# Two attention-and-MoE streams on one core: batch 1 projected while slot 0 loads, maxima of group 0 between the last expert blocks, results sent from two queues

## The reference

```python
x = x + 0.5 * ffn(layernorm(x))
x = x + attn(layernorm(x))        # 16 heads of 8, 4 kv heads, rotary
x = x + 0.5 * ffn(layernorm(x))

def ffn(x):
    x = x + softmax(q @ k.T / sqrt(8)) @ v @ w_proj     # q, k, v from layernorm(x) * w + b
    onehot = one_hot(argmax(layernorm(x) @ gate_w + gate_b), 8)
    return x + onehot-chosen expert: gelu(x @ w1[e]) @ w2[e]
```

## Time and profile before

| | |
|---|---|
| median of 3 runs | 1563.21 us (1561.63 to 1566.58) |
| the profiled execution | 1566.45 us |
| its span, first to last instruction | 1564.7 us |
| mean granted TensorE clock | 0.962 |
| busy: TensorE, VectorE, ACT, GpSimd | 1406.8, 1185.5, 1124.5, 639.8 us |

### The profile page before, as it was taken

One profiled execution on the slowest core, in us unless ns is written; L12 is line 12 of the kernel. 1 busy time (PEld: TensorE's weight loads), 2 busy tenths in 40 slices (PEclk: granted clock), 3 DMA queues, 4 the chain that ended last, 5 costly groups with the idle time before them and its releaser, 6 DMA issues.

```text
span 1564.7 us, 35538 instructions
## 1 busy us (share of the span) xinstructions
PE 1406.8 (90%) x12228; PEld 687.4 (44%) x12228; DVE 1185.5 (76%) x1945; ACT 1124.5 (72%) x2148; POOL 639.8 (41%) x972
## 2 busy tenths in 40 slices
PE   2899999999999886999999999999999999999895
PEld 1333334333339773333333333333334343334885
DVE  5788888888855254888888888888888888894532
ACT  1478887788785452778888887888887878787553
POOL 2422344542226555333544453233324543213753
PEclk8699999999999986999999999999999999999998
DMA  4344333533102315323322333332333233211243
GB/s 119 95 111 114 103 100 108 132 94 95 47 26 60 105 49 154 96 77 93 94 80 68 98 95 101 93 82 67 93 94 82 73 99 99 60 38 37 72 113 104
DMA packets 101423, 137.60 MB, mean 88 GB/s; under 512 B 29664, under 2 KB 72032, under 8 KB 101248
## 3 DMA queue, kind: packets, MB, share of 16 engines
q1 hardware_dynamic: 70864, 85.82, 19.1%
q0 software_dynamic: 24000, 45.04, 12.0%
q10 hardware_dynamic: 6384, 4.47, 1.0%
HBM read 79.05 MB, written 53.51 MB: 85 GB/s over the span
## 4 chain that ended last, share of the span: by engine, by line
PE 55%; DVE 31%; issue 6%; POOL 2%; DMA 2%; SPq 2%; ACT 1%; DVEq 0%; ACTq 0%; POOLq 0%
DVE maxima L1210 26%; PE banks L851 14%; PE banks L839 11%; PE banks L823 11%; PE banks L878 3%; PE banks L1554 3%; PE banks L860 3%; PE banks L1563 3%; PE banks L904 1%; PE banks L885 1%; SPq L463 1%; POOL by_token L1537 1%; DVE stats L1287 1%; DVE split L1218 1%; POOL sorted_x L691 1%
## 5 line engine op out<-in xcount | busy, mean ns | idle before, releaser
L1210 DVE TENSOR_REDUCE maxima<-banks 128x2 f32<-128x1024 f32 x768 | 924.2, 1222 | 171.9 <-PE banks L823 166.8
L1181 ACT ACTIVATE work<-banks 128x512 f32<-128x512 f32 x1536 | 829.3, 597 | 149.2 <-PE banks L839 135.2
L823 PE MATMUL banks<-K,Q 64*128 64x512 f32 x1536 | 572.7, 463 | 56.3 <-DVE maxima L1210 36.4
L839 PE MATMUL banks<-Q,K 64*128 64x512 f32 x1536 | 567.7, 451 | 0.6
L851 PE MATMUL banks<-work,V 128*9 128x256 f32 x6144 | 476.8, 382 | 1.6 <-ACT work L1181 0.8
L823 PEld LDWEIGHTS banks<-K,Q 64*128 64x128 f32 x1536 | 229.9, 190 | 214.6 <-DVE maxima L1210 126.4
L839 PEld LDWEIGHTS banks<-Q,K 64*128 64x128 f32 x1536 | 229.3, 186 | 181.7 <-issue 137.4
L851 PEld LDWEIGHTS banks<-work,V 128*9 128x9 f32 x6144 | 91.5, 88 | 276.1 <-issue 204.5
L710 POOL TENSOR_TENSOR lo<-full,hi 128x512 fp32r<-128x512 f32 x42 | 53.7, 1278 | 251.7 <-ACT hi L1059 144.4
L1617 DVE COPY work<-w 128x512 f32 x88 | 43.7, 497 | 87.2 <-PE banks L1554 75.5
L1563 PE MATMUL banks<-w,work 128*128 x736 | 102.3, 284 | 2.5 <-issue 1.3
(11 more groups left out here) (187 smaller groups left out, 1331.8 us busy)
## 6 DMA issues: line engine op xcount, KB each, us to landing
Q<-q_scratch SPq DMA_DIRECT2D x188, 128.0 KB, 2.6
K<-k_scratch SPq DMA_DIRECT2D x376, 64.0 KB, 2.4
Q<-zero_rows SPq DMA_DIRECT2D x182, 64.0 KB, 2.2
q_scratch<-hi POOLq DMA_DIRECT2D x42, 256.0 KB, 4.7
q_scratch<-lo POOLq DMA_DIRECT2D x42, 256.0 KB, 6.8
k_scratch<-hi POOLq DMA_DIRECT2D x21, 256.0 KB, 4.6
k_scratch<-lo POOLq DMA_DIRECT2D x21, 256.0 KB, 6.8
work<-sorted_x SPq DMA_DIRECT2D x76, 66.0 KB, 1.9
```

The costliest lines, as they stand in the source:

```text
L823: fill(nc.tensor.matmul(bank, q4[parts(j), n % SLOTS, j // 2, qt * P:(qt + 1) * P], k4[parts(j), n % SLOTS, j // 2, :], start=True, stop=T ...
L839: nc.tensor.matmul(scp[x % EXPS][:, :], k4[parts(j), n % SLOTS, j // 2, kt * P:(kt + 1) * P], q4[parts(j), n % SLOTS, j // 2, :], start=Tr ...
L1181: nc.scalar.activation(prob[:, kt, j ^ 1, :], scp[x % EXPS][:, :], ACT.Exp, scale=SCALE).then_inc(s.probs, 1)
L1210: nc.vector.tensor_reduce(c.maxima[:, at:at + 9:8], c.banks[:, k * S:(k + 2) * S].rearrange("p (m n) -> p m n", m=2), AX.X, ALU.max).then_ ...
```

## The change

**Opening of stream 0.** `BETWEEN` is gone: batch 1 is projected right behind batch 0 (`SECOND` in both streams), in tiles of its own (`apart(1)` now holds in both), and the maxima of group 0 close the opening. VectorE norms batch 1 ahead of the low parts of batch 0. Only slot 0 of `K`, `Q` and all of `V` are set in `setup`; the rest of `Q` and `K` and `empty` follow later. GpSimd, not ACT and SP, issues the straight loads of `K`. ACT issues its stores between its copies for batch 1. The statistics of batch 2 (`norms(-2, kt)`, first in VectorE's `main`) come behind the maxima of group 0, in both streams.

**Change of streams.** The maxima of group 0 of stream 1 move from behind the expert blocks into the opening's generator: one quarter ahead of each of the last three blocks, the fourth behind. SP clears and loads slot 0 from block 20 on.

**Finish.** VectorE adds half of Y to X during the last blocks; one pass for each batch is left. Loads and stores of the last four batches alternate between SP and ACT.

```diff
@@ setup, gpsimd
-            nc.gpsimd.memset(c.empty[:, :, :], 0.0)
-            nc.gpsimd.iota(c.empty[:, :, D].bitcast(U32), pattern=[[P, 2 * E]], base=NT * P, channel_multiplier=1)
+            nc.gpsimd.memset(c.V[:, :], 1.0)
+            nc.gpsimd.memset(cols(c.K, 0, KSLOT).bitcast(F32), -1.0)
@@ setup, vector
+            nc.vector.memset(cols(c.Q, 0, KSLOT).bitcast(F32), 0.0)
@@ Plan
-        for n, kt in SECOND if ahead else ():
+        for n, kt in SECOND:
             self.group(n, kt)
         self.maxima(0)
         for qt in range(QT):
             self.put([("max", 1, qt, j) for j in range(J)])
-            for n, kt in () if ahead else BETWEEN[qt]:
-                self.group(n, kt)
@@ sync, opening
-                    sp.wait_ge(c.q_clear, 1)
-                    sp.wait_ge(c.k_clear, 1)
...
-                    yield from pause(NBLK - RINGX)
+                    yield from pause(EARLY_AT + 16 - RINGX)
                     clear_rows(0)
                 whole_ready(sp, 0, 0)
                 yield from straight(sp, 0, 0)
-                for i in range(2):
+                for i in range(1 + label):
                     sp.wait_ge(s.lo[i], 1)
                     yield from straight(sp, i, 1)
@@ gpsimd, opening
-                    nc.gpsimd.memset(c.K[:, :].bitcast(F32), -1.0).then_inc(c.k_clear, 1)
-                    nc.gpsimd.memset(c.V[:, :], 1.0).then_inc(c.v_clear, 1)
+                    whole_ready(pool, 1, 0)
+                    yield from straight(pool, 1, 0)
+                    pool.wait_ge(s.lo[1], 1)
+                    yield from straight(pool, 1, 1)
+                    nc.gpsimd.memset(cols(c.K, KSLOT, (SLOTS - 1) * KSLOT).bitcast(F32), -1.0).then_inc(c.k_clear, 1)
+                    for i in range(2):
+                        low_part(i, 1)
+                    link(nc.gpsimd.memset(c.empty[:, :, :], 0.0))
+                    nc.gpsimd.iota(c.empty[:, :, D].bitcast(U32), ...).then_inc(c.empty_ready, 1)
@@ tensor, opening
-                for n, kt in FIRST + (SECOND if label else ()):
+                for n, kt in FIRST + SECOND:
                     group(n, kt)
                     if label:
                         yield
+                loaded(0)
+                for qt in range(QT):
+                    maxima(0, qt)
+                    if label:
+                        yield
@@ scalar, opening
+                if label == 0:
+                    group(-8, 0)
+                    roots(1)
+                    group(-8, 2)
+                    group(-6, 0)
+                    group(-6, 2)
+                    group(-4, 0)
+                    for i in range(2):
+                        yield from store(act, i, 0, s.first_stored[i], (0,))
+                    group(-4, 2)
+                    group(-2, 0)
+                    group(-2, 2)
@@ scalar, main
+                for i in range(2):
+                    stored(act, i, 2)
@@ vector, opening
-                    nc.vector.memset(c.Q[:, :].bitcast(F32), 0.0).then_inc(c.q_clear, 1)
+                    yield from early(1)
                     for i in range(2):
                         low_first(i)
-                    yield from early(1)
+                    nc.vector.memset(cols(c.Q, KSLOT, (SLOTS - 1) * KSLOT).bitcast(F32), 0.0).then_inc(c.q_clear, 1)
...
+                    yield from pause(4)
+                for qt in range(QT):
+                    for half in range(2):
+                        take_max(0, qt, half)
+                    if label:
+                        yield
@@ finish, vector
+        for b in range(B):
+            x, y = cols(c.X, b * S, S), cols(c.Y, b * S, S)
+            nc.vector.scalar_tensor_tensor(out=x, in0=y, scalar=0.5, in1=x, op0=ALU.mult, op1=ALU.add).then_inc(s.halved, 1)
+            yield
-            nc.vector.tensor_tensor(n, n, y, ALU.add).then_inc(s.summed, 1)
-            dve.wait_ge(s.summed, b + 1)
             nc.vector.scalar_tensor_tensor(out=x, in0=n, scalar=0.5, in1=x, op0=ALU.mult, op1=ALU.add)\
                 .then_inc(s.combined, 1)
```

More of the change, by code:

```diff
@@ L405, in apart @@
         def apart(b):
-            return label > 0 and b == 1
+            return b == 1
         def full(b):
@@ L638, in main @@
                             load_outputs(sp, c, b)
+                    if n == 1 and later:
+                        sp.wait_ge(c.empty_ready, 1)
                     if n >= 1 and later:
@@ L752, in main @@
                         norm(EARLY)
-                    if label and n < 0:
+                    if n < 0:
                         continue
@@ L1005, in main @@
                     pe.wait_ge(blocks.s.out_copied, HALVES * NBLK)
-                loaded(0)
-                for qt in range(QT):
-                    maxima(0, qt)
                 turn_max(0)
@@ L1012, in main @@
                     maxima(1, qt)
-                    for n, kt in () if label else BETWEEN[qt]:
-                        group(n, kt)
                 for n in range(last):
@@ L1145, in opening @@
                     yield from pause(EARLY_AT + 4)
-                for n, kt in FIRST:
-                    group(n, kt)
-                    if label:
-                        yield
-                group(-5, 0)
-                whole_ready(act, 1, 0)
-                if label == 0:
-                    act.wait_ge(c.k_clear, 1)
-                    yield from send_first()
-                else:
+                if label == 0:
+                    group(-8, 0)
[9 more added lines that the diff above has]
+                    group(-2, 2)
+                else:
+                    for n, kt in FIRST:
+                        group(n, kt)
+                        yield
+                    group(-5, 0)
+                    whole_ready(act, 1, 0)
                     sending = send_first()
@@ L1632, in finish, with send @@
 def finish(nc, c, ctx, out, blocks):
-    s = sems(ctx, nc, "fin", "summed combined stored")
+    s = sems(ctx, nc, "fin", "halved combined stored")
     ahead = B // HALVES
+    def send(eng, b):
+        eng.wait_ge(s.combined, b + 1)
+        eng.dma_start(out[b].rearrange("(t p) d -> p t d", p=P), by_token(cols(c.X, b * S, S))).then_inc(s.stored, 16)
     def sync(sp):
@@ L1643, in sync @@
         blocks.all_stored(sp, 4 * NBLK)
-        for b in range(ahead, B):
+        for b in range(ahead, B, 2):
             load_outputs(sp, c, b)
+        for b in range(ahead, B, 2):
+            send(sp, b)
     def vector(dve):
-        yield from pause(EARLY_AT)
+        for b in range(B):
+            x, y = cols(c.X, b * S, S), cols(c.Y, b * S, S)
+            nc.vector.scalar_tensor_tensor(out=x, in0=y, scalar=0.5, in1=x, op0=ALU.mult, op1=ALU.add).then_inc(s.halved, 1)
+            yield
         for b in range(B):
@@ L1661, in scalar @@
     def scalar(act):
-        yield from pause(EARLY_AT + 1)
-        for b in range(B):
-            if b == ahead:
-                yield from pause(NBLK)
-            elif b < ahead:
-                yield from pause(2)
-            act.wait_ge(s.combined, b + 1)
-            act.dma_start(out[b].rearrange("(t p) d -> p t d", p=P), by_token(cols(c.X, b * S, S))).then_inc(s.stored, 16)
+        yield from pause(RINGX + 1)
+        for b in range(ahead):
+            yield from pause(2)
+            send(act, b)
+        yield from pause(NBLK)
+        blocks.all_stored(act, 4 * NBLK)
+        for b in range(ahead + 1, B, 2):
+            load_outputs(act, c, b)
+        for b in range(ahead + 1, B, 2):
+            send(act, b)
         act.wait_ge(s.stored, 16 * B)
```

39 lines of the change are left out of this document (19 added, 20 removed).

## The result

The changed kernel takes 1556.16 us (median of 10 runs, 1553.59 to 1561.75), the kernel before beside it 1563.65 us (10 runs). The ratio is 0.9954, 95% interval 0.9939 to 0.9969: **faster, by 7.2 us**, where 20.5 were forecast.

A forecast was written before the change was run, and what follows sets the result against it. The chain was 55% TensorE, 31% VectorE; with steady steps unchanged, gains lay in waits at three places. 10.6 + 8.3 + 1.6 = 20.5 us off 1566.45 gave 1545.95, less 3.2 for the median: 1543, range 1538 to 1551.

The forecast's parts named there:

- Opening, up to the first max matmul: Start of stream 0: first max matmul at 29.8 in place of 34.45, 4.6 us earlier.
- The stall (2.8 us): Opening: batch 0's first tensor_scalar, 2.95 us long until GpSimd's memset of K ends, would lose 2.8 us.
- I keep the 5.5 us: Opening: from the last slot 0 load issue to the first max matmul, 5.5 us would pass as before.
- The check on TensorE: Opening: first max matmul can't precede the end of batch 1's matmuls, at 26.2 or up to 3 us later.
- Opening, from there to the first scores: First max matmul to the first exponential's scores: 21.2 us in place of 27.2, 6.0 us earlier.
- What could be late next: Opening: slot 1's stores go out earlier and have ten us of first maxima, so no wait was counted.
- ACT's wait: Opening: ACT waits for batch 1's stores before its first exponential; landed by 45, scores come at 51.
- Slot 1 sets it instead: Change of streams: slot 1's load sets group 1's start, 608.8 in place of 617.13, 8.3 us earlier.
- land 6.9 us later as before, plus 0.8: Change of streams: slot 1's scratch stores, out at 595.5, land at 603.2; 0.8 allows for 768 KB more beside GpSimd's.
- the stores still catch slot 0 or slot 1 at the change of streams: Rival: group 1 starts 3 us earlier, not 8; 15.2 us saved, 1548; chance 0.13.
- the one for the opening: Rival: slot 0 lands no earlier in the opening; 15.9 us saved, 1547; chance 0.14.
- both together: Slot 0 no earlier in the opening and stores catching a slot at the change of streams: 1553, chance 0.04.

The follow-up runs named there:

- after: The changed kernel itself, all three parts of the change, against the kernel before: 1556.16 us, ratio 0.9954.
- after_again: The changed kernel, unaltered, timed and traced a second time to learn the scatter: 1558.20 us, ratio 0.9963 to the kernel before.
- old_finish: The changed kernel with the finish of the kernel before (its order of loads and sums, ACT sending results): 1557.93 us, ratio 0.9957.
- old_transition: The changed kernel with the old change of streams: group 0's maxima behind all expert blocks, old pause before slot 0's load; 1573.08 us, ratio 0.9967.
- before: The kernel without the change, the base of all ratios: 1563.65 us.
- before_again: The kernel without the change, timed and traced a second time to learn the scatter: 1564.55 us, ratio 1.0005.
- act_late: hold_opening with ACT's three scratch stores of batch 0 issued behind all its copies for batch 1: 1567.29 us, ratio 0.9923 to the kernel before.
- hold_opening: The changed kernel, GpSimd issuing batch 1's six scratch stores in the opening only once batch 0's have landed: 1553.45 us, ratio 0.9931.
- hold_stats: hold_opening with VectorE's statistics of batch 2 ahead of the maxima of group 0: 1567.01 us, ratio 0.9925 to the kernel before.
- hold_both: hold_opening with batch 1's scratch stores also held at the change of streams until batch 0's have landed: 1562.36 us, ratio 0.9904.
- all: hold_both plus batch 2's statistics ahead of group 0's maxima, ACT's two q stores late, SP issuing the third: 1549.63 us, ratio 0.9913.

## Why the prediction was wrong, point by point

The direction was right. One wait in the opening was put at nothing, another at the change of streams was named and sized too small, and the sum came out too large by a factor of two and a half or more. Means over the traces that share an order give the sizes:

| part | forecast | in the traces | how |
|---|---|---|---|
| opening | 10.6 | 4.8 | first scores 61.4 (two traces) to 56.6 (after, after_again, old_finish, old_transition) |
| change of streams | 8.3 | 2.2 | block 19's end to first scores 32.4 (before, before_again, old_transition) to 30.2 (the six with the new order and the stores beside) |
| finish | 1.6 | 1.0 | see old_finish |
| sum | 20.5 | 8.0 | the timed ratios, 0.9954 and 0.9963, make 7.2 and 5.8 us |

**Opening, up to the first max matmul (4.6 forecast).** It came 3.65 us earlier in the pair profiled, about 3.1 over all traces. The stall (2.8 us) went, the setup cost nothing that shows (the turn of batch 0 is 2.67 us earlier), GpSimd issued eight `K` parts in 4.7 us, not 6.0, and VectorE's memset of `Q` did not hold it: both ran side by side from 19.8 to 23.3. But the sentence "ACT's three stores and SP's lie beside them again, so I keep the 5.5 us" kept a wait that the stores cause: act_late took 5.7 us off it. The 5.5 us themselves came again (from 25.13, the end of SP's last issue, to 30.80), but behind another part: the last to land was `Q` low, whose issue the stores had slowed, not `K`. That the forecast of this point was off by no more than 1.0 to 1.6 us is in part luck. (The check on TensorE took ACT's copy of v to be over at 21.6; that row begins at 21.53 and lasts 0.60. It changes nothing, as TensorE was through with batch 1 at 25.2.)

**Opening, from there to the first scores (6.0 forecast).** This step failed. It read "What could be late next: slot 1, but its scratch stores go out earlier ... and it has the ten us of the first maxima". Measured 24.7 to 26.7 us and not 21.2, and 3.3 to 5.3 us of that is the wait for slot 1. The stores of batch 0 do go out earlier. But batch 1's six stores were moved from 59.5 to 28.3, where batch 0's are still in flight: the sum moved batch 1's projection and left its transfers out. It gave batch 1's stores ten us to land, for ACT's wait, and never asked the same of batch 0's. hold_opening shows this: with them held, 21.4 us, the 21.2 forecast within 0.2. The statistics, sized at 1.2 us, took 1.4 where hold_stats moves them.

**Change of streams (8.3 forecast).** "Slot 1 sets it instead" named the right wait. The term that failed is "land 6.9 us later as before, plus 0.8", with the 5.6 us behind it. The 6.9 us run from the end of SP's last store issue, of `k_scratch`, to the clear of slot 1. But that clear waits for `q_scratch` (SP's waits in the trace of before, 575 to 622 us):

```profile
SPq L567 <- DMA q_scratch<-lo: 6.8, 1, 6.8
```

So it is not the landing of the store it was read from. Taken by the prediction's own two intervals:

| | forecast | before, before_again, old_transition | the six with the new order and the stores beside | the four with both held |
|---|---|---|---|---|
| SP's last store issued to clear of slot 1 | 7.7 | 5.7 to 7.8 | 8.5 to 13.8, mean 10.9 | 4.9 to 5.8 |
| clear to group 1 | 5.6 | 5.6 to 6.9 | 7.2 to 8.5, mean 7.9 | set by the turn in three |

The two make 18.9 us in the mean for the 13.3 of the sum: 5.6 us. In the new order GpSimd's and SP's stores leave together, where before the change most of GpSimd's went out some 10 us ahead of SP's; that this is why they land later fits these numbers. hold_both, with GpSimd's held, brings the first interval to 5.8 us and group 1 to 14.2 us after the first max matmul, near the 13.2 of the sum (11.1, "1.2 for the statistics, 0.9 for split and turn"). About 0.9 us more was a baseline from one trace: the 24.1 us from block 19's end to group 1 were 22.6 in before_again and 22.9 in old_transition. And slot 0, early in the trace of after, was 7 us late in that of after_again. So the rival "the stores still catch slot 0 or slot 1 at the change of streams", to which I gave 0.13, is what happened. Slot 1 held by stores in the opening stood in no rival; the one for the opening was about slot 0. The measured 1556 lies beyond every rival that had a gain: even "both together" stood at 1553.

**Finish (1.6 forecast).** The last pass ends 1.55 us earlier, as computed. I took the way from the last pass to the end as fixed; it was 5.2 to 5.3 us in the three traces with the old finish and 5.8 to 6.0 in the ten with the new one. Probably this is because the results now come in pairs and the four stores to the output leave within 2.6 us; no run takes that apart.

**Steady steps** didn't differ: from the first scores of stream 1 to its expert stage 811.7 and 810.7 us before, 811.4 and 811.9 after. From the first scores of stream 0 to the end of block 19 they were 531.4 and 530.9 before, 531.8 and 529.0 after, so this stretch too differs by up to 3 us between executions of one kernel.

**What stays open.** The traced parts sum to 8.0 us and the runs give 5.8 to 7.2; the scatter of the change of streams alone, up to 5 us between executions, covers that. That slot 0 is 7 us late in one execution and in time in the next goes with how far GpSimd's stores overlap SP's `K` issues: in four of the six kernels the stores began within 0.3 us of the end of these issues, and TensorE had slot 0 2.9 to 3.7 us behind it; in hold_stats they overlapped by 0.7 us, and it was 5.5; in after_again by 1.7 us, and it was 8.4. In hold_both, with no such stores, it was 3.9. The overlap was not tried by itself. Nor was an order tried that holds batch 1's stores until the maxima's transfer into `Q` is out, which would show whether the 1.3 to 4.2 us lost behind group 1 can be had as well.

The version that beats both is hold_both: the changed kernel, with batch 1's scratch stores held until batch 0's have landed in both streams. It is 1.0% faster than the kernel before, and 0.5% faster than the change. The ratios don't tell it from the other held kernels with the new order, 0.9908 to 0.9931.

## What to carry to other kernels

When a computation is moved earlier, its transfers move too: list the bytes that will be in flight in the new place, and size the landing of every store that someone waits for from a row with as much beside it, not from a quiet one. A transfer that nobody waits for soon should wait for the one that is waited for; a semaphore wait on an engine that has nothing else to do was worth about as much here as the whole reordering. Then look at what the held transfer meets when it does go out. And where a place scatters by 5 us between executions of one kernel, take its baseline from several traces before forecasting a gain of 8.

## What the runs showed of the hardware

- A 256 KB store to memory that slot 1 waited for at the change of streams landed 8.2 to 9.1 us after its issue with batch 1's stores held (the chains of four kernels), 13.8 to 16.2 us with them issued together with batch 0's (six kernels), and 10.4 and 11.0 us in the old order, where most of them had gone out some 10 us ahead (before_again and old_transition).
- ACT's stores slow SP's loads though both issue on their own: in the opening, SP issued four 32 KB transfers into slot 0 in 2.81 us with ACT's stores out of the way (act_late and all) and in 3.81 to 6.53 with them beside (nine kernels). The first max matmul, which waits for them, came 5.7 us later in hold_opening than in act_late.
- GpSimd issued eight transfers in 4.7 us while VectorE's 3.47 us memset ran; the exclusion that held the `tensor_scalar` for 2.95 us did not appear between these two. VectorE's casts in `setup` were held, 2.37 us for 0.18, until GpSimd's memsets beside them ended. By the Trainium skill's page "SBUF — State Buffer", section "Who interferes with whom", a VectorE instruction with at most one SBUF input, outside the two-port modes, does not contend with GpSimd, with no exception for a memset on this chip; the rows of the memset agree.
